# Edge features in a fused four-layer graph network: one transpose for two node columns, and edge matmuls of 256 columns behind the node matmuls

## The reference, cut to what matters

```python
x = _layernorm(x + _L0_gnn_ref(...), axis=-1)     # its last product, h1 @ W2 + b2, is in the third stage too
x = _layernorm(x + _L1_gnn_ref(...), axis=-1)
# _L1_gnn_ref
sums = jax.ops.segment_sum(edge_attr, src, num_segments=n)          # 64 features an edge
edge_attr_agg = sums / jnp.maximum(counts, 1.0)[:, None]
combined = jnp.concatenate([x, edge_attr_agg, u_expanded], axis=1)  # 256 + 64 + 128
h = jax.nn.relu(combined @ W1 + b1)                                 # 512 hidden
return h @ W2 + b2                                                  # 256
```

## Time and profile before

| | |
|---|---|
| median of 3 runs | 6238.54 us |
| the profiled execution's own time | 6242.73 us |
| its span, first to last instruction | 6240.2 us |
| PE busy | 4395.5 us (70%) |
| VectorE busy | 3753.9 us (60%) |
| GpSimd busy | 3687.1 us (59%) |
| ScalarE busy | 1988.6 us (32%) |
| PE in the slices of the third stage | 99% and more |
| mean granted TensorE clock | 0.853 |

### The profile page before, as it was taken

One profiled execution on the slowest core, in us unless ns is written; L12 is line 12 of the kernel. 1 busy time (PEld: TensorE's weight loads), 2 busy tenths in 40 slices (PEclk: granted clock), 3 DMA queues, 4 the chain that ended last, 5 costly groups with the idle time before them and its releaser, 6 DMA issues. The chain is left out here.

```text
span 6240.2 us, 71314 instructions
## 1 busy us (share of the span) xinstructions
PE 4395.5 (70%) x16758; PEld 2857.5 (46%) x16758; DVE 3753.9 (60%) x10131; ACT 1988.6 (32%) x3345; POOL 3687.1 (59%) x3371
## 2 busy tenths in 40 slices
PE   1566649989999999999997777577772000566665
PEld 0344425556666666666665666555552000222222
DVE  1344435656666666666664677577775554565665
ACT  0111125532222222222222222277772000444444
POOL 2378854445555555555555677477777776555554
PEclk5777769999999999999999888799996555777777
DMA  9977779953333333333332444399994332666665
GB/s 359 378 150 140 130 184 365 365 199 111 122 116 118 120 112 123 114 119 120 114 124 72 128 127 131 112 304 304 306 303 135 92 92 88 235 227 228 228 227 190
DMA packets 497942, 1125.26 MB, mean 180 GB/s; under 512 B 165814, under 2 KB 248714, under 8 KB 497814
## 3 DMA queue, kind: packets, MB, share of 16 engines
q1 hardware_dynamic: 346380, 913.22, 42.2%
q0 software_dynamic: 113184, 174.84, 11.8%
q10 hardware_dynamic: 38250, 35.85, 1.9%
HBM read 623.20 MB, written 543.83 MB: 187 GB/s over the span
## 5 line engine op out<-in xcount | busy, mean ns | idle before, releaser
L1437 PE MATMUL psum<-arena,ident 128*128 128x512 f32 x784 | 554.9, 875 | 379.7 <-DVE psum L1604 238.8
L942 PE MATMUL psum<-arena,W1b 128*128 128x512 f32 x1568 | 725.3, 605 | 0.0
L965 PE MATMUL psum<-W2b,arena 128*128 128x256 f32 x3136 | 725.2, 379 | 0.0
L730 DVE TENSOR_SCALAR arena<-arena 128x256 f32<-128x256 f32 x784 | 462.3, 650 | 302.1 <-POOL arena L725 302.1
L536 PE MATMUL psum<-arena 128*128 128x324 f32 x980 | 370.3, 547 | 367.1 <-DVE arena L456 248.2
L965 PEld LDWEIGHTS psum<-W2b,arena 128*128 128x128 f32 x3136 | 573.1, 190 | 66.3 <-issue 0.5
L855 ACT ACTIVATE arena<-psum,hbias 128x512 f32<-128x512 f32 x392 | 269.3, 687 | 860.2 <-PE psum L942 860.2
L1437 PEld LDWEIGHTS psum<-arena,ident 128*128 128x128 f32 x784 | 209.6, 279 | 724.3 <-issue 479.4
L1425 PE MATMUL psum<-Wg,arena 128*128 128x264 f32 x1568 | 399.5, 411 | 174.0 <-ACT arena L1481 174.0
L1081 POOL DMA_INDIRECT tab<-arena,IDX x392 | 398.8, 1017 | 175.3 <-issue 88.4
L1520 POOL DMA_INDIRECT ad_d<-arena,FE x392 | 425.5, 1086 | 113.2 <-issue 113.2
(11 more groups left out here) (207 smaller groups left out, 9046.2 us busy)
## 6 DMA issues: line engine op xcount, KB each, us to landing
arena<-tab SPq DMA_DIRECT2D x194, 544.0 KB
arena<-in_x SPq DMA_DIRECT2D x194, 512.0 KB, 4.6
x_d<-arena SPq DMA_DIRECT2D x194, 512.0 KB, 7.5
arena<-x_d SPq DMA_DIRECT2D x194, 512.0 KB, 5.3
tab<-zero SPq DMA_DIRECT2D x132, 486.0 KB
tab<-blank SPq DMA_DIRECT2D x97, 544.0 KB
h_d<-arena SPq DMA_DIRECT2D x97, 528.0 KB, 4.6
arena<-h_d SPq DMA_DIRECT2D x97, 528.0 KB, 4.3
```

Of the source, the lines that this page charges most:

```text
L730: v.tensor_scalar(y[:, j, :], r[:, j, :], self.mv[:, j, 0:1], self.rs[:, j:j + 1], ALU.subtract, ALU.mult).then_inc(self.s["y"], 1)
L942: last = pe.matmul(psum[:, BR + c % RING, :], W1b[:, f, c * P:(c + 1) * P], x1T[:, f, :], start=False, stop=(f == FH - 1))
L965: last = pe.matmul(outB(j), hid[:, c, j * P:(j + 1) * P], W2b[:, c, :], start=(c == 0), stop=(c == KH - 1))
L1437: last = pe.matmul(psum[:, b + i, :], ident[:, :], a[:, k.slot(2), 2 * i:2 * i + 2, :].rearrange("p j d -> p (j d)"), start=(n == 0), stop ...
```

## The change

`em` holds the edge features once, `[2, J, DE]`. A transpose now takes two node columns side by side (64 features of column 2i and 64 of column 2i + 1), so `tr_e` has two transposes instead of four, and `eT` (`[J // 2, P]`) has the features of the even node columns at partitions 0 to 63 and of the odd ones at 64 to 127. Its copy has 256 columns. A chunk's edge part is therefore two matmuls, one for the even node columns (a = 0, lower 64 rows) and one for the odd (a = 1, upper 64 rows), each of 256 columns and each into its own half of the bank in strips of 128. The node matmuls come first in each bank (`start=True`), the edge matmuls behind them. The new order on TensorE is: nodes 0 and 1; the edge pair (0, even) and (1, odd); nodes 2; a wait; the pair (0, odd) and (1, even); three columns of `mmA`; the wait for the first relu; nodes 3; the pair (2, even) and (3, odd); the last column of `mmA`; a wait; the pair (2, odd) and (3, even); then the transposes and `mmB` as before. The two waits are on a new semaphore `half` which TensorE's own edge matmuls count up. The `mmA` sequence is the same in itself, cut in two.

```diff
-        em = take([2, J, 2, DE])
+        em = take([2, J, DE])
-        eT = take([STEP])
+        eT = take([J // 2, P])
@@ p3_scalar, evac
-                act.activation(eT, psum[:, BT, :], ACT.Copy).then_inc(p3["T"], 1)
+                act.activation(eT, psum[:, BT, 0:STEP // 2].rearrange("p (i n) -> p i n", n=P), ACT.Copy).then_inc(p3["T"], 1)
@@ p3_vector, first
-                v.tensor_tensor(out=em[:, k.b, :, :, :], in0=p3e[:, k.b, :, 0:DE].rearrange("p j (a d) -> p j a d", a=1).to_broadcast([P, J, 2, DE]),
-                                in1=rc.rearrange("p (j a d) -> p j a d", a=1, d=1).to_broadcast([P, J, 2, DE]), op=ALU.mult).then_inc(p3["em"], 1)
+                v.tensor_tensor(out=em[:, k.b, :, :], in0=p3e[:, k.b, :, 0:DE],
+                                in1=rc.rearrange("p (j d) -> p j d", d=1).to_broadcast([P, J, DE]), op=ALU.mult).then_inc(p3["em"], 1)
@@ p3_tensor
-            def mmA(k):
+            def mmA(k, columns=range(J)):
...
-                for j in range(J):
+                for j in columns:
@@ tr_e
-                for j in range(J):
-                    last = pe.transpose(psum[:, BT, j * P:(j + 1) * P], em[:, k.b, j, :, :].rearrange("p a d -> p (a d)"), ident[:, :])
+                for i in range(J // 2):
+                    last = pe.transpose(psum[:, BT, i * P:(i + 1) * P], em[:, k.b, 2 * i:2 * i + 2, :].rearrange("p a d -> p (a d)"), ident[:, :])
...
-            def edges(c):
-
-                h = (c % 2) * DE
-                pe.matmul(psum[:, BR + c % RING, :], W1e[h:h + DE, c * P:(c + 1) * P], eT[h:h + DE, :], start=True, stop=False)
             def nodes(c):
                 for f in range(FH):
-                    last = pe.matmul(psum[:, BR + c % RING, :], W1b[:, f, c * P:(c + 1) * P], x1T[:, f, :], start=False, stop=(f == FH - 1))
-                last.then_inc(p3["hidw"], 1)
-
-            def hidden(k):
-                pe.wait_ge(p3["T"], (FH + 1) * (k.s + 1))
-                wait(pe, p3["hidr"], KH * k.s)
-                edges(0)
-                edges(1)
-                nodes(0)
-                nodes(1)
-                pe.wait_ge(p3["hidr"], KH * k.s + 1)
-                edges(2)
-                edges(3)
-                nodes(2)
-                nodes(3)
+                    pe.matmul(psum[:, BR + c % RING, :], W1b[:, f, c * P:(c + 1) * P], x1T[:, f, :], start=(f == 0), stop=False)
+
+            def edges(c, a, done):
+
+                h = a * DE
+                o = psum[:, BR + c % RING, :].rearrange("p (i a n) -> p i a n", a=2, n=P)[:, :, a, :]
+                return pe.matmul(o, W1e[h:h + DE, c * P:(c + 1) * P], eT[h:h + DE, :, :], start=False, stop=done)
@@ body
-                hidden(k)
+                pe.wait_ge(p3["T"], (FH + 1) * (k.s + 1))
+                wait(pe, p3["hidr"], KH * k.s)
+                nodes(0)
+                nodes(1)
+                edges(0, 0, False).then_inc(p3["half"], 1)
+                edges(1, 1, False).then_inc(p3["half"], 1)
+                nodes(2)
+                pe.wait_ge(p3["half"], KH * k.s + 2)
+                edges(0, 1, True).then_inc(p3["hidw"], 1)
+                edges(1, 0, True).then_inc(p3["hidw"], 1)
                 if live(k.plus(2), NS):
-                    mmA(k.plus(2))
+                    mmA(k.plus(2), range(J - 1))
+                pe.wait_ge(p3["hidr"], KH * k.s + 1)
+                nodes(3)
+                edges(2, 0, False).then_inc(p3["half"], 1)
+                edges(3, 1, False).then_inc(p3["half"], 1)
+                if live(k.plus(2), NS):
+                    mmA(k.plus(2), range(J - 1, J))
+                pe.wait_ge(p3["half"], KH * k.s + 4)
+                edges(2, 1, True).then_inc(p3["hidw"], 1)
+                edges(3, 0, True).then_inc(p3["hidw"], 1)
```

More of the change, by code:

```diff
@@ L750, in gnn_program @@
         p3 = {k: sem(f"p3_{k}") for k in ("y", "xb", "mmA", "rA", "mx", "rc", "em", "tr", "T", "hidw", "hidr",
-                                          "x1b", "mmB", "rB")}
+                                          "x1b", "mmB", "rB", "half")}
         p3_h = [sem(f"p3_h{b}") for b in range(2)]
```

## The result

The changed kernel takes 6341.11 us (median of 6 runs, 6336.01 to 6342.6) against 6239.45 for the one before: ratio 1.0161, 95% interval 1.0148 to 1.0174, 1.6% slower. The profiled execution took 6340.31 us, with a span of 6337.9. The forecast was 6338.

The account below looks back on a forecast made before the run. PE was taken to bound the stage: +0.80 for blocks, -0.22 for transposes, +0.41 for the relu stall and +0.01 make +1.00 us a step, +98 us over 98 steps, and +2: 6338 us, range 6288 to 6382.

Parts of the forecast that it names:

- PE as the bound: Third stage: a microsecond on PE is one of the kernel; work on ACT, DVE or POOL costs nothing until PE waits.
- Two more blocks, +0.80 us: Edge pairs on PE: four blocks a step instead of two, each with 0.40 us fixed cost, +0.80 us a step.
- Rivals C and D: Block's fixed cost: C, cheap row-form switch, 6179 us at zero, chance 0.04; D, only weight loads hidden, 6250, chance 0.04.
- Two transposes less, -0.22: Edge transposes on PE: two fewer at 0.109 us each, counted in full, -0.22 us a step.
- Eight increments at nothing: Semaphore increments on a step's eight edge matmuls: no charge, against 0.21 us a step by the Trainium skill's estimate.
- The stall on the relu, +0.41: mmB's start waits for chunk 2's relu: 1.05 us needed, 0.64 covered by PE work, +0.41 us a step.
- Rival A: Only the blocks cost, the relu being covered by something unseen: +0.59 us a step, 6298 us, chance 0.08.
- PE's busy share: PE in the third stage: busy a little under 98%, no longer 500 of 500 us.
- The `half` waits at nothing: PE's two waits on its own edge matmuls: 0 where covered, some 0.2 us each without the second's mmA cover.
- Rival E: Half waits empty PE, each costing about 0.20 us: 39 us in all, 6377 us, chance 0.07.
- The last two steps: Steps without mmA pay about 0.85 us each for the first relu; with the half waits, +2 us once.
- em at half its time: DVE's product for em halves from 2.63 us, with no effect on the kernel's time.

Follow-up runs that it names:

- e6: Changed kernel plus three further em-size products on VectorE and one further 256-column copy on ScalarE each step, into unread tiles: 6348.24 us, ratio 1.0173.
- e4: Kernel before, with its duplicated features and four transposes, but four hidden-chunk banks and the four 512-column edge matmuls in one block: 6201.59 us, ratio 0.9939.
- e3: Changed kernel with four hidden-chunk banks, all node matmuls first, then all eight edge matmuls in one block, then all of mmA: 6185.93 us, ratio 0.9915.
- e5: Changed kernel with its two edge transposes done twice, thus four as before: 6360.52 us, ratio 1.0194.
- e7: Changed kernel with only one increment of half for each first pair, by its second matmul: 6341.92 us.
- e1: Changed kernel with mmA cut into two columns, one and one, the last column behind the fourth edge pair: 6300.64 us, ratio 1.0097.
- e2: Changed kernel with edge pairs put together two by two, only the half wait between them, nodes 2 and all of mmA moved ahead: 6336.19 us, ratio 1.0157.
- e8: Changed kernel with both matmuls of each edge pair in the same row half, so they can't run side by side: 6463.07 us.

## Why the prediction was right

- **PE as the bound** holds: of the stage's growth of 101.2 us, 97 are the growth of PE's step (0.99 us) 98 times. Another 2.5 lie in the last two steps and 1.5 in the first, both below; the prediction had 98, 2 and nothing for the three. Work added elsewhere (e6) leaves the step at 22.05.
- **Two more blocks, +0.80 us.** The step that carried most doubt, since no row showed a block of 256 columns, was right: a block takes 0.63 us to what follows it, and its fixed cost beyond its passes is 0.40 in all. e4 shows the 0.40 by taking one away, and e3, with four pairs in one block at one fixed cost, that it belongs to the switch of the row form and not to the pair. Rivals C and D (the loads or the whole of it hidden) fall: the load of the first edge matmul still starts with the block, at 2509.66.
- **Two transposes less, -0.22.** e5 gives it back: 22.27 - 22.05.
- **Eight increments at nothing.** With all eight the step is 22.05, where the sum had 22.06 without a charge for them and would have 22.27 with the 0.21 that the prediction works out from the Trainium skill; e7 takes two away without effect.
- **The stall on the relu, +0.41.** In the trace 0.39, in e1 0.41. Rival A fell: its cover does not exist. One sign was misjudged: PE's busy share is 99.1% (495.75 of 500) and not a little under 98%, since only 0.19 of the stall is idle time in its record.
- **The `half` waits at nothing.** Right for the 96 steps with mmA: no such wait in the rows of the middle. Rival E fell. Its price of 0.20 was too low for a bare wait, though: 0.26 until the load starts and the load's own 0.11 (e2).
- **The last two steps.** +2 us was too little by 0.5, and made up of other parts. From its start to the next step's start the last step but one takes 19.52 us where it took 17.60; the last, to the start of its last mmB block, 11.88 where it was 9.29. That is 4.51 more, 2.5 beyond twice the 0.99. Each has a wait of 0.83 us for the first relu, as said. The second `half` wait is bare in each, at 0.37 and not 0.20, but as no mmA stands between its two pairs they are one block, and a switch of 0.40 goes: together that adds nothing. What the prediction left out is that in the last step no transposes stand between the block and mmB: none are saved there, and mmB's relu is bare, with PE idle for 0.86 us.
- **The first step.** The prediction has no term for it. Its first node group, eight records at the stage's start, took 5.04 us (1336.02 to 1341.06) instead of 3.52. The granted clock was 0.50 (1.2 GHz, the lower level) in 1336 to 1338, where a record takes 0.85 us instead of 0.43, and 1.00 from 1339 on. Just before, PE had done only transposes, with idle stretches between them as it waited for ScalarE's copies. In the kernel before, with two edge transposes more at that place, the clock stayed at 1.00. The same group is slow in e1, e3, e7 and e8 too, and not in e2, e5 (transposes done twice) or e6; what decides it stays open.
- **em at half its time** was wrong, in size only and without effect: the product took 2.36 us in the middle of the stage, from 2.63. The copy L849 did fall, from 0.60 to 0.38.

The ends of the stage in the changed kernel, and a window of the kernel before for its first step (in the windows the clock is the third number from the end):

```profile
1336.02 5.12 PE L937 MATMUL psum<-arena,W1b 128*128 128x512 f32 x8 [0.47 <-ACT arena L849]
...
1336.00:1338.00 2.00, 1.99 (x3) 0.95 (x4) 0.69 (x2) 1.37 (x2) 1.27 (x1) 0.50 0.00 0
...
3461.80 1.98 PE L937 MATMUL psum<-arena,W1b 128*128 128x512 f32 x4 [0.83 <-ACT arena L855]
...
3485.60 7.14 PE L952 MATMUL psum<-W2b,arena 128*128 128x256 f32 x32 [0.86 <-ACT arena L855]
```
```profile
1342.00:1345.00 3.00, 3.00 (x10) 1.22 (x7) 2.30 (x6) 1.27 (x3) 0.63 (x1) 1.00 0.06 8
```

The point on em has its rows in the changed kernel, the product at the stage's start and in the middle, and GpSimd's sum:

```profile
1325.21 0.42 DVE L878 TENSOR_TENSOR arena<-arena 128x256 f32<-128x256 f32 x1
...
2514.18 2.36 DVE L878 TENSOR_TENSOR arena<-arena 128x256 f32<-128x256 f32 x1
```
```profile
2513.90 2.35 POOL L805 TENSOR_TENSOR arena<-arena,b2b 128x1024 f32<-128x1024 f32 x1 [1.26 <-DVE arena L730]
```

GpSimd's sum begins 0.28 us ahead of VectorE's product and ends at 2516.25; the product ends at 2516.54, 0.29 after it. It is not 2.36 us of work: at the stage's start, with no such sum beside it, the same product took 0.42, and in e6 it took 2.37 beside the sum and 0.41 behind it. So most of the time in the record is waiting inside the instruction, and halving the columns shortens only the rest: 2.63 - 2.36 is 0.27, as is 0.69 (the 128x512 product at the stage's start, before the change) - 0.42. The Trainium skill ("SBUF — State Buffer", Who interferes with whom) says that a VectorE instruction with two inputs in SBUF contends with a GpSimd instruction that reads SBUF, since they share a read port, and that whichever starts first has it for its whole instruction. The trace agrees as far as the product ends only behind the sum; it ends 0.29 us behind it, though, less than its 0.42 alone. A duration that was recorded beside such an instruction of another engine should not be scaled by size.

## What to carry to other kernels

Count what a switch of the row form costs before splitting narrow matmuls: here 0.40 us each time PE went from 128-row to 64-row matmuls and back, whatever stood inside. Put all matmuls of one form into one block, if banks allow it; a bank that is idle at that moment may be the one that is missing. When the order on the bounding engine changes, look at what now stands between the last producer and the first consumer: a column of mmA on the wrong side of the last block cost 0.41 us a step, and moving it back cost nothing.

## What the runs showed that I had not expected

PE waiting bare for its own matmul costs about as much as the whole switch there and back: 0.37 us against 0.40 (e2). The prediction had 0.2 for it; the 0.36 was worked out only ahead of e2. Sixteen 64-row records of alternating halves stream two by two at 0.216 us a pair of records, with all loads but the first covered (e3): inside the row form nothing is lost, even with two waits on PE's own semaphore among them, as long as each looks back a pair further. And the stage's first step lost 1.5 us to a granted clock of 0.50, which no term of the sum had.
